# Zero matmuls in TensorE's waits, more expert blocks ahead of the turned weights, and a store in four pieces

## The reference

```
x = x + gnn0(layernorm(x), adj)    # 3 attention heads over adj, two GRU cells
x = x + ffn0(layernorm(x))         # 1 shared + 8 routed experts, hidden 512, gelu, top 2
x = x + gnn1(layernorm(x), adj)    # bilinear weights (16 parts), adj @ x, relu
x = x + ffn1(layernorm(x))         # 8 routed experts, hidden 256, relu, top 2
```

## Time and profile before

| | |
|---|---|
| median of 3 timed runs | 2057.66 us |
| profiled execution's own time | 2052.76 us |
| its span, first to last instruction | 2051.0 us |
| TensorE busy | 1805.9 us, 88% |
| VectorE busy | 1641.0 us, 80% |
| ScalarE busy | 1351.6 us, 66% |
| GpSimd busy | 203.4 us, 10% |
| mean granted clock of TensorE | 0.927 |

### The profile page before, as it was taken

One profiled execution on the slowest core, in us unless ns is written; L12 is line 12 of the kernel. 1 busy time (PEld: TensorE's weight loads), 2 busy tenths in 40 slices (PEclk: granted clock), 3 DMA queues, 4 the chain that ended last, 5 costly groups with the idle time before them and its releaser, 6 DMA issues.

```text
span 2051.0 us, 28337 instructions
## 1 busy us (share of the span) xinstructions
PE 1805.9 (88%) x8959; PEld 872.3 (43%) x9108; DVE 1641.0 (80%) x1431; ACT 1351.6 (66%) x1498; POOL 203.4 (10%) x154
## 2 busy tenths in 40 slices
PE   1531979999999999999997999999988899997997
PEld 1521434444444444444446444444453344454443
DVE  7655679888989898989567787777868988856998
ACT  6876148787887887887244656655546877735775
POOL 0000002000001011001440000000007900000000
PEclk7555999999999999999996999999999999988999
DMA  9996056655555555455400311111002089913221
GB/s 386 410 421 232 32 169 205 203 155 167 149 153 171 153 152 179 143 152 158 175 0 1 105 52 41 51 41 41 1 25 120 0 336 428 417 46 105 102 101 65
DMA packets 94319, 309.77 MB, mean 151 GB/s; under 512 B 15513, under 2 KB 52857, under 8 KB 80399
## 3 DMA queue, kind: packets, MB, share of 16 engines
q1 hardware_dynamic: 94242, 308.79, 42.8%
HBM read 295.78 MB, written 12.98 MB: 151 GB/s over the span
## 4 chain that ended last, share of the span: by engine, by line
PE 52%; DVE 3%; ACT 2%; issue 2%; POOL 0%; ACTq 0%; DVEq 0%; POOLq 0%
PE psum L1145 13%; PE psum L1157 13%; PE psum L1230 8%; PE psum L1093 8%; PE psum L1208 2%; PE psum L1118 1%; PE psum L1120 1%; PE psum L921 1%; DVE prod L1778 1%; PE psum L927 1%; PE psum L1132 1%; PE psum L916 1%; PE psum L1122 1%; PE psum L1123 1%; ACT prod L869 1%
## 5 line engine op out<-in xcount | busy, mean ns | idle before, releaser
L738 ACT ACTIVATE ss<-KR,cls 128x1024 bf16<-128x1024 int16 x384 | 412.9, 1138 | 103.2 <-DVE pl L1602 102.3
L1093 PE MATMUL psum<-ph,Tt 128*128 128x512 bf16 x1503 | 411.1, 380 | 11.4 <-DVE pl L1602 9.8
L825 ACT ACTIVATE hid<-psum,fB 128x1024 f32<-128x1024 f32 x208 | 227.3, 1112 | 184.0 <-PE psum L1145 184.0
L1145 PE MATMUL psum<-hTp,fW 128*128 (+1 forms) x1202 | 284.5, 382 | 12.4 <-ACT hid L825 4.6
L1157 PE MATMUL psum<-hidp,fW 128*128 128x512 bf16 x1241 | 279.4, 379 | 2.3 <-DVEq L1744 1.9
L1599 DVE TENSOR_TENSOR ph<-ss,Ahi 128x3072 bf16<-128x3072 bf16 x128 | 228.8, 1788 | 54.3 <-PE psum L1093 50.0
L1722 DVE TENSOR_TENSOR hidp<-hid,hidp 128x1024 bf16<-128x1024 f32 x208 | 245.4, 1222 | 26.6 <-ACT hidp L819 26.4
L1093 PEld LDWEIGHTS psum<-ph,Tt 128*128 128x128 bf16 x1536 | 149.8, 98 | 193.9 <-issue 9.0
L1602 DVE TENSOR_TENSOR pl<-ss,Alo 128x3072 bf16<-128x3072 bf16 x128 | 227.3, 1776 | 0.0
L1093 PE MATMUL psum<-pl,Tt 128*128 128x512 bf16 x753 | 225.7, 380 | 0.8
L1145 PEld LDWEIGHTS psum<-hTp,fW 128*128 128x128 bf16 x1248 | 117.1, 98 | 168.9 <-ACT hid L825 32.2
(11 more groups left out here) (233 smaller groups left out, 2053.9 us busy)
## 6 DMA issues: line engine op xcount, KB each, us to landing
Ar<-in_adjT SPq DMA_DIRECT2D x64, 1024.0 KB, 11.5
Ab<-in_adjT SPq DMA_DIRECT2D x128, 512.0 KB, 3.9
A<-in_adjT SPq DMA_DIRECT2D x32, 2048.0 KB, 10.7
mB<-mk_d SPq DMA_DIRECT2D x64, 512.0 KB, 3.6
Tt<-T_d SPq DMA_DIRECT2D x128, 192.0 KB, 2.3
Tt<-Tn_d SPq DMA_DIRECT2D x128, 64.0 KB, 2.0
T_d<-tb SPq DMA_DIRECT2D x32, 192.0 KB, 1.9
RD<-rden_d SPq DMA_DIRECT2D x12, 512.0 KB, 5.1
```

Of the source, the lines that this page charges most:

```text
L738: last = nc.scalar.activation(ss[s % 2][:, h, :], KR[:, h, rb * RB:(rb + 1) * RB], ACT.Sigmoid, scale=STEP, bias=cls[:, ds(t * HEADS + h, 1)])
L825: nc.scalar.activation(hid[j % HB][:, :], flat[:, j % 2 * CW:j % 2 * CW + CW], func, bias=fB1[:, j:j + 1]).then_inc(act_done[k], 1)
L1093: last = nc.tensor.matmul(psum[:, 2 * h + q, :], Tt[s % AS][:, h, w, :], mv[:, q * CH:(q + 1) * CH], start=fresh and k == 0, stop=False, s ...
L1145: last = nc.tensor.matmul(psum[:, j % 2 * 2 + b, :], fW[0][x][:, j * P:(j + 1) * P], hTp[y][:, ds(q * CW + b * CH, CH)], start=(w == 0), s ...
```

## The change

Three places get matmuls of zeros: 26 in the norm k = 0 ahead of the last slice's mean, 4 in each norm ahead of the 32 transposes, and `cleared(0)` is done five times over. In the expert stages TensorE does 2 (k = 0) or 4 (k = 1) up blocks ahead of the turning, ScalarE 8 activations, and VectorE the split of the first `lag` blocks ahead of the shares; TensorE's first chunk becomes straight code. The output is stored by chunks of 1024 nodes, each when its chunk is summed.

```diff
--- before.py
+++ after.py
@@ -501,9 +501,10 @@
                     sp.wait_ge(l_lo, 4 * i + s - 3)
                     sp.dma_start(A4[s][:, :], adj[ds((4 * i + s) * P, P), :]).then_inc(l_in[s], 16)
             ffn_loads(1, *FFN1)
-            sp.wait_ge(dve_ffn1, NW * 2 * NE)
-            sp.dma_start(out, xT[:, :]).then_inc(out_done, 16)
-            sp.wait_ge(out_done, 16)
+            for q in range(NW):
+                sp.wait_ge(dve_ffn1, (q + 1) * 2 * NE)
+                sp.dma_start(out[:, wide(q)], xT[:, wide(q)]).then_inc(out_done, 16)
+            sp.wait_ge(out_done, 16 * NW)
             sp.wait_ge(spilled, 32)
 
 
@@ -833,17 +834,19 @@
                     hidden(0, j)
                 act.wait_ge(r_sel, 3 * k + 2)
                 nc.scalar.activation(rs[:, 3, :], rs[:, 2, :], ACT.Exp).then_inc(r_exp, 1)
+                for j in range(HB, 2 * HB):
+                    hidden(0, j)
                 for b in range(4):
                     act.wait_ge(r_tr, 4 * k + b + 1)
                     half = N // 2 + b % 2 * (N // 4)
                     nc.scalar.activation(mk8[:, b * N // 4:(b + 1) * N // 4], flat[0:NE, half:half + N // 4],
                                          ACT.Copy).then_inc(r_mk8, 1)
                 with act.Fori(0, NW - 1) as q:
-                    for j in range(HB, nE * nF):
+                    for j in range(2 * HB, nE * nF):
                         hidden(q, j)
-                    for j in range(HB):
+                    for j in range(2 * HB):
                         hidden(q + 1, j)
-                for j in range(HB, nE * nF):
+                for j in range(2 * HB, nE * nF):
                     hidden(NW - 1, j)
 
             ffn_weights(0, *FFN0)
@@ -910,6 +913,9 @@
             for q in range(NC):
                 if k == 0:
                     pe.wait_ge(g_nin, 2 * NC + (1 if q < 4 else 2))
+                    if q == NC - 1:
+                        for _ in range(26):
+                            nc.tensor.matmul(psum[:, q, :], zero[:, 0:P], zero[:, :], start=True, stop=True)
                     pe.wait_ge(g_used, 2 * q + 4)
                 if k == 2:
                     pe.wait_ge(l_add, q + 1)
@@ -922,6 +928,8 @@
                                             mean[:, 0:1], start=(q == 0 and t == 0), stop=True,
                                             skip_group_check=True)
                 last.then_inc(lt_sum, 1)
+            for _ in range(4):
+                nc.tensor.matmul(psum[:, 7, :], zero[:, 0:P], zero[:, :], start=True, stop=True)
             pe.wait_ge(ln_normed, 3 + k)
             for t in range(NT):
                 last = nc.tensor.transpose(flat[:, t * P:(t + 1) * P], stat[:, 4, t:t + 1].to_broadcast([P, P]),
@@ -994,9 +1002,10 @@
 
             with pe.Fori(0, groups) as g:
                 def cleared(hf):
-                    for q in range(hf * NC // 2, (hf + 1) * NC // 2):
-                        nc.tensor.matmul(psum[:, q, :], zero[:, 0:P], zero[:, :], start=True, stop=False,
-                                         skip_group_check=True)
+                    for r in range(1 if hf else 5):
+                        for q in range(hf * NC // 2, (hf + 1) * NC // 2):
+                            nc.tensor.matmul(psum[:, q, :], zero[:, 0:P], zero[:, :], start=r == 0, stop=False,
+                                             skip_group_check=True)
 
                 def selected(q):
                     pe.wait_ge(lv_clean, 2 * NC * g + 2 * q + 2)
@@ -1161,7 +1170,8 @@
                     last.then_inc(down_done[k], 1)
 
                 pe.wait_ge(r_sel, 3 * k + 1)
-                for e in range(lag):
+                ahead = lag + (1, 2)[k]
+                for e in range(ahead):
                     up(0, e)
                 pe.wait_ge(r_sel, 3 * k + 3)
                 for t in range(NT):
@@ -1172,7 +1182,11 @@
                     if t % 8 == 7:
                         last.then_inc(r_tr, 1)
                 pe.wait_ge(r_mk8, 4 * k + 4)
-                with pe.Fori(0, NW - 1) as q:
+                for e in range(nE):
+                    if e + lag >= ahead:
+                        up((e + lag) // nE, (e + lag) % nE)
+                    down(0, e)
+                with pe.Fori(1, NW - 1) as q:
                     for e in range(nE):
                         up(q + (e + lag) // nE, (e + lag) % nE)
                         down(q, e)
@@ -1697,14 +1711,17 @@
                         c.link(V.scalar_tensor_tensor(out=lg[:, :, :], in0=s1[:, :, :], scalar=-1e30,
                                                       in1=lg[:, :, :], op0=ALU.mult, op1=ALU.add))
                 V.tensor_tensor(rs[:, 2, :], rs[:, 1, :], rs[:, 0, :], ALU.subtract).then_inc(r_sel, 1)
-                dve.wait_ge(r_exp, k + 1)
-                c.link(V.tensor_scalar(rs[:, 5, :], rs[:, 3, :], 1.0, None, ALU.add))
-                c.link(V.reciprocal(rs[:, 6, :], rs[:, 5, :]))
-                c.link(V.tensor_tensor(rs[:, 7, :], rs[:, 6, :], rs[:, 3, :], ALU.mult))
-                c.link(V.tensor_tensor(s1[:, :, :], s1[:, :, :], rs[:, 6, :].unsqueeze(2).to_broadcast(T), ALU.mult))
-                c.link(V.tensor_tensor(s2[:, :, :], s2[:, :, :], rs[:, 7, :].unsqueeze(2).to_broadcast(T), ALU.mult))
-                V.tensor_tensor(s1[:, :, :], s1[:, :, :], s2[:, :, :], ALU.add).then_inc(r_sel, 1)
-
+
+                def shares():
+                    dve.wait_ge(r_exp, k + 1)
+                    c.link(V.tensor_scalar(rs[:, 5, :], rs[:, 3, :], 1.0, None, ALU.add))
+                    c.link(V.reciprocal(rs[:, 6, :], rs[:, 5, :]))
+                    c.link(V.tensor_tensor(rs[:, 7, :], rs[:, 6, :], rs[:, 3, :], ALU.mult))
+                    c.link(V.tensor_tensor(s1[:, :, :], s1[:, :, :], rs[:, 6, :].unsqueeze(2).to_broadcast(T),
+                                           ALU.mult))
+                    c.link(V.tensor_tensor(s2[:, :, :], s2[:, :, :], rs[:, 7, :].unsqueeze(2).to_broadcast(T),
+                                           ALU.mult))
+                    V.tensor_tensor(s1[:, :, :], s1[:, :, :], s2[:, :, :], ALU.add).then_inc(r_sel, 1)
 
                 def high(q, e):
                     def hi(j):
@@ -1753,6 +1770,7 @@
 
                 for e in range(lag):
                     high(0, e)
+                shares()
                 with dve.Fori(0, NW - 1) as q:
                     chunk(q, True)
                 chunk(NW - 1, False)
```

## The result

The changed kernel takes 2040.76 us (median of 4 runs, 2040.19 to 2041.66), the kernel before, beside it, 2057.05 (4 runs, 2055.0 to 2057.7): ratio 0.9922 [0.9906, 0.9938]. Forecast were 11.2 us and 2046.5 (range 2041.5 to 2052.5). The direction was right, the gain was larger by 5 us. Against the single profiled execution of before the forecast comes out almost exactly: 2052.76 to 2041.66, 11.1 us.

What follows compares the result with a forecast made beforehand. TensorE was taken as the bound (52% of the span in the chain of waits), with gains where it is not full. Terms summed to 11.2 us, taking the median from 2057.66 to 2046.5, range 2041.5 to 2052.5.

Steps and rivals of the forecast that it cites:

- Levels: Start of the levels: 5 x 4 clearing zeros instead of 4 raise the clock for the tile matmuls; 1.1 us gained.
- 26 zeros: First norm, ahead of the last mean matmuls: column sums run faster, but VectorE's weight split lets only 1.4 us through.
- 4 zeros: Ahead of each norm's 32 transposes: 0.6 us gained in the bilinear norm, 0.3 in the second expert norm, none in the first.
- First stage: First expert stage: up block 1 ahead of the turned weights brings the first down block sooner; 2.4 us, bounds 1.0 and 3.2.
- Second stage: Second expert stage: blocks 2 and 3 ahead; first down block 0.9 later, 2.6 us more work behind it; 1.7 gained.
- Store: Output in four pieces: only a last 512 KB piece lands after VectorE ends; 3.7 us gained, upper bound 4.4.
- one table load back (1124.7): First expert stage: after the Exp, ScalarE loads a table once more, until 1124.7, before its activations ahead of the mask copies.
- The base: Savings worked out in the profiled execution of 2052.76 us were taken off the timed median of 2057.66, giving 2046.5.
- (a): Rival: clocks bring nothing on the path, all four zero terms are eaten; 7.8 us left, 2049.9; chance 0.20.
- (b): Rival: zeros raise no clock and stand in the way; 2.0 and 4.8 lost, 7.8 gained, 2056.7, no change; chance 0.06.
- (c): Rival: more than forecast; first norm stays warm through transposes and router (3 more), first stage gets 3.2; 2042.7; chance 0.12.
- (d): Rival: the peeled first chunk's straight code feeds instructions too slowly, 25 ns a matmul, 15.6 us lost; 2062.1; chance 0.04.

## Why the prediction was wrong

By its own steps:

* **Levels**, 1.1 forecast. The tile matmuls start at 2.4 GHz as said. The stage is 1.4 us shorter against the profile of before, 2.2 against the mean of the 8 profiles without these zeros: that profile was the shortest of them. The 2.2 come through: from the first tile matmul to the GRU cells the means are 779.8 and 777.6. Mis-sized by its base.
* **26 zeros**, 1.4 forecast, 1.6 measured from the means to the transposes. The limit was named rightly, VectorE's split: the sums took 10.98, not 8.7, and it covered that. What may have been given back: the transposes and router behind them took 17.7 in the mean of 7 profiles, 16.1 in 9 without; one short time among the 7, six among the 9. That is no proof, and the medians of the two kernels that differ by these zeros point the other way.
* **4 zeros**, 0.6 and 0.3; 0.5 in the mean and nothing measured (second sums to up block 27.8 and 27.9). That the clock falls in the bilinear sums ahead of them (3 us in the profile of after) was not thought of; it happens with and without zeros.
* **First stage**, 2.4 forecast, 2.3 in this profile, 3.0 in the mean, with the wait of 3.15 us for ScalarE where some 3 were expected.
* **Second stage**, 1.7 forecast, 0.9 in this profile, 2.3 in the mean of 8. The first down block came 1.7 later (0.9 said) and the rest was 2.6 shorter as said; in the other seven profiles it came between 0.6 sooner and 1.4 later.
* **Store**, 3.7 forecast, 3.6 to 3.8 measured in every profile with it. Right.
* **The failed step**: "one table load back (1124.7)". I counted the load that the change adds ahead of the copies, and not the ones that it takes from ScalarE's loop. Rows 7 show the Exp's load at 1121.92 and nothing of the loop's, and I priced the loops by windows at 1450 and 1950. The first lies in the last chunk of the first stage, in straight code; the second lies in the loop of the second stage, where the only load is the Exp's at 1867.48, ahead of the loop. The loop of the first stage, the only one with the load, was in neither. The sum put these loads at nothing; they are worth 2.5 us.
* **The base.** Savings were worked out in an execution of 2052.76 and taken off a median of 2057.66 one for one. The 4.9 us between them were noted and not asked after. They are clock that the median run loses and that one didn't: against the means of the table it is shorter by 0.8 at the levels, 1.3 at the GRU cells, 0.9 at the router, 0.8 at the bilinear means and 1.5 at their sums, 5.3 in all. The changed kernel's profile is, the other way round, at the upper end of its runs (2038.45 to 2042.09).

By the means, 2.2 + 1.6 + 0.5 + 3.0 + 2.6 + 2.3 + 3.6 = 15.8 us, against 16.3 between the medians; with the router's 1.6 taken off as a loss, 14.2. Between these two it is not settled. Of the 4.6 us between 11.2 and 15.8, 2.6 are the table loads, 1.1 the levels, 0.6 the second stage and 0.6 the first; the small rest cancels.

That the two profiles differ by the forecast's 11.1 is luck. The seven terms give 11.1 in this pair and the table loads 2.5 more. The router takes 2.8 and the bilinear sums 2.9 back. About 3.3 more come from stretches that are in no row: up to the first tile matmul, the attention, and the bilinear stage, 1.0 to 1.2 us each.

The rivals: (a) falls, zeros alone bring 3.1 us [0.8 to 5.4]. (b) falls by the clock of 1.00 right behind the levels' zeros, and by the ratios of the change and of the zeros alone. (c) is nearest by its time, 2042.7, but not by its mechanism: from the first norm's transposes through the router it took 18.0, longer than before, and the first stage gave 2.3, not 3.2. (d) falls: from 1150 to 1200, in the peeled chunk, TensorE is busy for 50.00 us with 230 matmuls, as from 1250 to 1400 in the loop.

On the Trainium skill's rule that transposes don't count as busy ("TensorE: Matmul & The Clock Gate", part 4): the profile of after shows again what the earlier trace rows show. In its first norm the transposes start at 1091.79, the stretches up to 1097 have 0.50, 1097 to 1098 has 0.54 and 1098 to 1099 has 1.00, and until 1098.31 TensorE runs nothing else. No kernel here isolates the transposes.

## What to carry to other kernels

Look at what state a hardware loop is entered in: a ScalarE table load inside the body is paid in every pass, and one activation of one column ahead of the loop takes it out. Read the full stretch of each loop, not its last pass, when pricing it. Before savings are taken off a median, ask how the profiled execution differs from it: here 0.927 against 0.924 of granted clock was 5 us, as large as the error of the forecast.

## What the runs showed of the hardware

* In the loop of the first expert stage each table load (1.28 us) made TensorE wait 1.25 or 1.26 us; a one-column Gelu ahead of the loop took the loads out of it.
* The same wait of 2.84 us ahead of the GRU cells is followed by a granted clock of 1.00 in one execution and 0.50 in another; the cells then take 82.5 or 85.5 us.
* Matmuls of zeros raise the granted clock: at the levels it rises in 203 to 204 while nothing else runs on TensorE, it is 1.00 in the first full microsecond of the work, and the stage takes 76.7 us in all nine profiles that have them, 78.1 to 79.6 without.
* TensorE can be busy without a gap and still fall to 1.2 GHz: in the 128x1 fp32 sums of the bilinear norm (64 in 11.61 us) the clock has 0.67 in 1514 to 1515.
* A GpSimd subtraction of 128x4608 from SBUF held VectorE's 0.69 us instructions for 9.31 and 9.27 us. The Trainium skill ("SBUF — State Buffer", on who interferes with whom) says that a VectorE instruction with two SBUF inputs contends with a GpSimd instruction that reads SBUF, and calls the shared port pair an exclusive lock; this trace agrees.
